# Value-side matrix of a cross-attention: fp16 high and low halves with three products in place of each fp32 product

## The reference, cut to what matters

```
vh = heads_split(v @ Wv)                 # v = ctx_1024, (2, 77, 256); 16 heads of 64
attn = softmax(dots)                     # dots: 1024 rows of each batch against 77 keys
out = einsum('bhij,bhjd->bhid', attn, vh)
out = out.transpose(0, 2, 1, 3).reshape(b, n, h * d)
out = out @ Wo + bo                      # Wo: (1024, 256)
```

## Time and profile before

| what | value |
|---|---|
| median of 3 runs | 427.75 us (427.56 to 428.26) |
| the profiled execution's own time | 428.12 us |
| its span, first to last instruction | 426.3 us |
| TensorE (PE) busy | 404.8 us, 95% of the span |
| VectorE (DVE) busy | 277.7 us, 65% |
| ScalarE (ACT) busy | 252.2 us, 59% |
| GpSimd (POOL) busy | 244.9 us, 57% |
| mean granted TensorE clock | 0.987 |

### The profile page before, as it was taken

How to read it: one execution, slowest core, us unless ns; L and a number is a source line. 1 busy time by engine, 2 the same in 40 slices (tenths; PEclk the granted TensorE clock), 3 DMA queues, 4 the chain that set the end, 5 groups by cost and what they waited for, 6 DMA issues and landing times.

```text
span 426.3 us, 10134 instructions
## 1 busy us (share of the span) xinstructions
PE 404.8 (95%) x3176; PEld 307.6 (72%) x3176; DVE 277.7 (65%) x684; ACT 252.2 (59%) x443; POOL 244.9 (57%) x213
## 2 busy tenths in 40 slices
PE   8899899999999999786999999999999999999991
PEld 8677577788877887674677777777777777777771
DVE  1777889899899989979688955444444444444340
ACT  3759889999899948444556444444444444444430
POOL 6536879998998865444054535445444444544242
PEclk9999999999999999989899999999999999999997
DMA  8992356566575624438767998888999888988753
GB/s 266 364 325 62 123 148 207 161 181 197 158 235 162 184 82 158 144 113 175 162 119 133 148 137 130 137 145 139 139 144 144 143 143 142 123 144 149 116 77 37
DMA packets 106241, 66.03 MB, mean 155 GB/s; under 512 B 80977, under 2 KB 99281, under 8 KB 106193
## 3 DMA queue, kind: packets, MB, share of 16 engines
q1 hardware_dynamic: 98512, 54.90, 55.2%
q0 software_dynamic: 7680, 10.49, 16.0%
HBM read 36.23 MB, written 9.96 MB: 108 GB/s over the span
## 4 chain that ended last, share of the span: by engine, by line
PE 58%; issue 16%; DMA 9%; DVE 6%; POOLq 3%; POOL 3%; ACT 2%; DVEq 0%; ACTq 0%
PE ps L816 14%; PE ps L648 12%; PE ps L618 11%; DMA out_rows<-work,idx_all 9%; PE ps L836 7%; PE ps L631 4%; POOLq L1707 3%; POOL work L1698 3%; PE ps L520 2%; PE ps L613 2%; PE ps L587 1%; PE ps L664 1%; PE ps L532 1%; DVE work L1136 1%; PE ps L602 1%
## 5 line engine op out<-in xcount | busy, mean ns | idle before, releaser
L816 PE MATMUL ps<-w_all,work 128*128 x960 | 151.4, 314 | 2.3 <-issue 2.3
L816 PEld LDWEIGHTS ps<-w_all,work 128*128 128x128 f16 x960 | 94.3, 99 | 48.9 <-issue 2.4
L1719 POOL DMA_INDIRECT out_rows<-work,idx_all x40 | 64.1, 1602 | 105.2 <-ACT work L1073 101.8
L1511 DVE SCALAR_TENSOR_TENSOR work<-ps,work 128x352 f32<-128x352 f32 x80 | 41.3, 523 | 66.9 <-PE ps L816 66.8
L836 PE MATMUL ps<-w_all,work 128*128 x681 | 80.8, 273 | 0.0
L836 PEld LDWEIGHTS ps<-w_all,work 128*128 128x128 f16 x681 | 66.4, 98 | 10.7 <-issue 0.2
L1636 POOL TENSOR_TENSOR w_all<-stage,w_all 128x1088 f16<-128x1088 f32 x30 | 67.6, 2256 | 9.2 <-ACT w_all L910 8.6
L1052 ACT ACTIVATE work<-ps 128x352 f32<-128x352 f32 x80 | 36.8, 463 | 54.0 <-PE ps L816 53.9
L1058 ACT ACTIVATE work<-work 128x704 f16<-128x704 f32 x39 | 30.8, 790 | 62.4 <-DVE work L1511 62.4
L1698 POOL DMA_INDIRECT work<-xn_rows,idx_all x40 | 41.2, 1029 | 29.0 <-issue 10.2
L618 PE MATMUL ps<-w_all 128*128 128x462 f16 (+1 forms) x288 | 57.4, 336 | 0.0
(11 more groups left out here) (159 smaller groups left out, 537.9 us busy)
## 6 DMA issues: line engine op xcount, KB each, us to landing
stage<-in_wt SPq DMA_DIRECT2D x36, 544.0 KB, 4.5
work<-in_x SPq DMA_DIRECT2D x30, 128.0 KB, 3.6
out_rows<-work SPq DMA_DIRECT2D x18, 128.0 KB, 4.4
xn_rows<-work SPq DMA_DIRECT2D x18, 128.0 KB, 4.4
w_all<-in_x SPq DMA_DIRECT2D x1, 1536.0 KB, 14.7
work<-work SPq DMA_TRANSPOSE x78, 3.7
w_all<-in_wk SPq DMA_DIRECT2D x2, 512.0 KB, 5.2
w_all<-in_wq SPq DMA_DIRECT2D x4, 256.0 KB, 7.0
```

What stands on the lines that cost most here:

```text
L816: mm = pe.matmul(ps[:, c, 0:half], xt[:, t % 2, block, :], weights(wbase + off, half), start=(k == 0 and n == 0), stop=(k == KD - 1 and n ...
L1511: dve.scalar_tensor_tensor(out=sg[:, t % 2, cols], in0=ps[:, 2 + c, 0:HID // 2], scalar=1.0 / SP_W, in1=sg[:, t % 2, cols], op0=ALU.mult, ...
L1719: pool.indirect_dma_start(out=acc, out_offset=bass.IndirectOffsetOnAxis(ap=idx_all[:, t:t + 1], axis=0), in_=yb[:, t % 2], in_offset=None, ...
```

## The change

The head values are kept as fp16 high and low halves `vz_h` and `vz_l`, in the bytes that `vz` had, and the output weights as `wo_h` and `wo_l` (64 times the weight, as fp16 high and low half). A product of B is then three fp16 products, high x high, low x high and high x low, issued one after the other. ScalarE rounds both halves of a pair (`v_high`, two instructions in place of one), VectorE subtracts for both (`v_low`, two instructions in place of one copy). ScalarE makes `wo_high(0)`, `wo_high(1)` (128 x 1024 each) and scales the bias in place, VectorE makes `wo_low(0)`, `wo_low(1)`. The scale 64 goes out of `b_high` and `b_low`. In step 0 of ScalarE `x_high(1)` stands ahead of `w_high(0)`.

```diff
         kt, o = pview(o, [PAIRS, B * J], F32)
-        vz, o = pview(o, [3, B, HJP], F32)
+        vz, _ = pview(o, [3, B, HJP], F32)
+        vz_h, o = pview(o, [3, B, HJP], F16)
+        vz_l, o = pview(o, [3, B, HJP], F16)
+        wo_h, o = pview(o, [INNER // P, D], F16)
+        wo_l, o = pview(o, [INNER // P, D], F16)
...
                 pe.wait_ge(wv_in[m // (PAIRS // 2)], 16)
-                for r in range(2):
-                    at_least(pe, v_half[r], m - 2)
+                at_least(pe, vl_ok, 2 * (m - 2))
                 head_values(wv_sb, m, V_BANKS[m % 3])
...
-                return pe.matmul(b_bank(k)[:, b], vz[rows, m % 3, b, cols], wo_sb[rows, m, :], start=start, stop=stop,
-                                 skip_group_check=True)
+                pairs = ((vz_h, wo_h), (vz_l, wo_h), (vz_h, wo_l))
+                for n, (v, w) in enumerate(pairs):
+                    mm = pe.matmul(b_bank(k)[:, b], v[rows, m % 3, b, cols], w[rows, m, :], start=(start and n == 0),
+                                   stop=(stop and n == len(pairs) - 1), skip_group_check=True)
+                return mm
...
-                for half in range(2):
-                    pe.wait_ge(wo_in[half], 16)
-                    pe.wait_ge(v_half[half], PAIRS)
+                pe.wait_ge(wo_lo_ok, 2)
+                pe.wait_ge(vl_ok, 2 * PAIRS)
                 even, odd = b_terms(2 * g, 0), b_terms(2 * g + 1, 1)
                 if g == 0:
-                    pe.wait_ge(bo_in, 16)
+                    pe.wait_ge(bo_ok, 1)
...
-            def v_even(m):
-                rows, j0 = slice(0, DH), head_col(2 * m)
+            def v_high(m):
                 act.wait_ge(kv_mm, PAIRS + m + 1)
-                act.activation(vz[rows, m % 3, :, j0:j0 + J],
-                               ps[rows, V_BANKS[m % 3], 0:B * J].rearrange("p (b j) -> p b j", b=B),
-                               ACT.Copy).then_inc(v_half[0], 1)
+                for r in range(2):
+                    rows, j0 = slice(r * DH, (r + 1) * DH), head_col(2 * m + r)
+                    act.activation(vz_h[rows, m % 3, :, j0:j0 + J],
+                                   ps[rows, V_BANKS[m % 3], 0:B * J].rearrange("p (b j) -> p b j", b=B),
+                                   ACT.Copy).then_inc(vh_ok, 1)
+
+            def wo_high(g):
+                act.wait_ge(wo_in[g], 16)
+                act.activation(wo_h[:, 4 * g:4 * g + 4], wo_sb[:, 4 * g:4 * g + 4], ACT.Copy, scale=SP_B).then_inc(wo_hi_ok, 1)
+
+            def bo_scale():
+                act.wait_ge(bo_in, 16)
+                act.activation(bo_b[:], bo_b[:], ACT.Copy, scale=SP_B).then_inc(bo_ok, 1)
...
                 if n == 0:
+                    wo_high(0)
+                    wo_high(1)
+                    bo_scale()
+                    x_high(1)
                     w_high(0)
-                    x_high(1)
                     b_high(0)
...
-            def v_odd(m):
-                rows, j0 = slice(DH, P), head_col(2 * m + 1)
-                dve.wait_ge(kv_mm, PAIRS + m + 1)
-                dve.tensor_copy(vz[rows, m % 3, :, j0:j0 + J],
-                                ps[rows, V_BANKS[m % 3], 0:B * J].rearrange("p (b j) -> p b j", b=B)).then_inc(v_half[1], 1)
+            def v_low(m):
+                for r in range(2):
+                    rows, j0 = slice(r * DH, (r + 1) * DH), head_col(2 * m + r)
+                    dve.wait_ge(vh_ok, 2 * m + r + 1)
+                    dve.tensor_tensor(vz_l[rows, m % 3, :, j0:j0 + J],
+                                      ps[rows, V_BANKS[m % 3], 0:B * J].rearrange("p (b j) -> p b j", b=B),
+                                      vz_h[rows, m % 3, :, j0:j0 + J], ALU.subtract).then_inc(vl_ok, 1)
+
+            def wo_low(g):
+                dve.wait_ge(wo_hi_ok, g + 1)
+                dve.scalar_tensor_tensor(out=wo_l[:, 4 * g:4 * g + 4], in0=wo_sb[:, 4 * g:4 * g + 4], scalar=SP_B,
+                                         in1=wo_h[:, 4 * g:4 * g + 4], op0=ALU.mult, op1=ALU.subtract).then_inc(wo_lo_ok, 1)
...
-                    dve.scalar_tensor_tensor(out=b_lo[:, :, c, :], in0=b_bank(k), scalar=SP_B, in1=b_hi[:, :, c, :],
-                                             op0=ALU.mult, op1=ALU.subtract).then_inc(b_lo_ok, 1)
+                    dve.tensor_tensor(b_lo[:, :, c, :], b_bank(k), b_hi[:, :, c, :], ALU.subtract).then_inc(b_lo_ok, 1)
...
             for m in (6, 7):
-                v_odd(m)
+                v_low(m)
+            for g in range(2):
+                wo_low(g)
```

More of the change, by code:

```diff
@@ L262, in build @@
         vz_ok, kv_mm, k_ok = (sem(n) for n in ("vz_ok", "kv_mm", "k_ok"))
-        v_half = sems("v_half", 2)
+        vh_ok, vl_ok, wo_hi_ok, wo_lo_ok, bo_ok = (sem(n) for n in ("vh_ok", "vl_ok", "wo_hi_ok", "wo_lo_ok", "bo_ok"))
         a_mm, a_hi_ok, a_lo_ok = sem("a_mm"), sem("a_hi_ok"), sem("a_lo_ok")
@@ L891, in b_high @@
                 for k in (2 * g, 2 * g + 1):
-                    act.activation(b_hi[:, :, B_CHUNKS[k], :], b_bank(k), ACT.Copy, scale=SP_B).then_inc(b_hi_ok, 1)
+                    act.activation(b_hi[:, :, B_CHUNKS[k], :], b_bank(k), ACT.Copy).then_inc(b_hi_ok, 1)
             def normalise(i):
@@ L1017, in _ @@
                 key_pair(m)
-            v_even(0)
+            v_high(0)
             normalise(0)
             key_pair(3)
-            v_even(1)
+            v_high(1)
             normalise(1)
@@ L1025, in _ @@
                 key_pair(m)
-                v_even(m - 2)
+                v_high(m - 2)
             for m in (6, 7):
-                v_even(m)
+                v_high(m)
             for n in range(NT):
@@ L1480, in _ @@
                 a_low(m)
-            v_odd(0)
+            v_low(0)
             a_low(3)
-            v_odd(1)
+            v_low(1)
             x_low(0)
@@ L1486, in _ @@
                 a_low(m)
-                v_odd(m - 2)
+                v_low(m - 2)
             for m in (6, 7):
-                v_odd(m)
+                v_low(m)
+            for g in range(2):
+                wo_low(g)
             dve.wait_ge(xall_in[1], 16)
```

## The result

The changed kernel is slower: 433.29 us median of 17 runs (430.04 to 434.63) against 428.54 of 17 runs of the kernel before (425.06 to 433.63), ratio 1.0116 with the interval 1.0088 to 1.0144. The forecast was 427.6 and no change, in a range of 427.2 to 429.0. The means of all 17 runs, 432.99 and 429.78, are 3.2 us apart, the medians 4.75.

What follows compares the result with a forecast made beforehand. Ahead of 48 us a chain of waits between TensorE, ScalarE and VectorE was taken to bound the kernel, then TensorE. Terms +0.20 + 0.10 - 0.42 = -0.12 us gave a 427.6 us median, range 427.2 to 429.0.

Steps and rivals of the forecast that it cites:

- The sum: Path terms at the end of the chain: +0.20 + 0.10 - 0.42 = -0.12 us.
- the preparation: Extra work ahead of make_b(0): +0.20 us for ScalarE's second v_high instruction, +0.10 for make_b(0) waiting for VectorE's wo_low.
- The products: TensorE's products of B: a pair falls from 0.432 to 0.327 us, saving 0.42 in make_b(0); other savings mostly hidden.
- The rival of a strict order: TensorE's products run in program order: a pair takes 0.436 us, make_b(0) costs 0.1 more; 428.15 us, chance 0.07.
- The upper bound, 0.40: VectorE's 64 x 154 subtraction ahead of make_b(0): one bounded between 0.24 and 0.40 us, 0.24 taken.
- The rival at 0.35: VectorE is late: subtractions cost 0.35 us, wo_low ends at 27.5, +0.35 on the sum; 428.0 us, chance 0.12.
- The wait ahead of L631: Sign that the forecast is right: this wait grows to over 2 us.
- the rival that I gave 0.25: TensorE's clock falls from 45.7 or 47.16 us on, losing 0.9 to 1.6 us, 1.2 taken; 428.8 us, chance 0.25.
- Carrying to the end: From 47.28 us on TensorE works without a gap that counts, so a shift there is carried to the end.

Runs made afterwards that it cites:

- the moved preparation: The changed kernel with its gaps filled and its preparation on ScalarE and VectorE reordered: 427.74 us; the same with three later gaps filled too: 427.66 us.
- the filled kernel: The changed kernel plus 40 small unused TensorE products behind make_b(4) and 16 ahead of prob_turn(0)'s last two transposes: 427.82 us, ratio 0.9982.

## Why the prediction was wrong, step by step

Two steps of it failed. The sum put the clock at nothing: what was saved in `make_b(3)` and `make_b(4)` "becomes idle time ahead of 45.11 and 47.28", and this idle time was taken to be free in the forecast, while it brought the clock to half speed for 6.8 us and cost 1.9 us in the trace. And the preparation was priced at +0.30, where it took 1.55.

- **The products: right.** Halves of the rows go on lying beside each other, -0.42 forecast for `make_b(0)`, -0.51 measured, and 1.44 of the saving of `make_b(3)` and `make_b(4)` hidden. The rival of a strict order wanted at least 1.85 us there (four pairs of 0.436 and one step more). The rule of the Trainium skill behind it ("TensorE: Matmul & The Clock Gate", Part 3), that matmuls start and end in program order, does not hold between the two halves of the rows here: 24 products of 0.109 in 1.49 us.
- **The preparation: too small by a factor of five.** I had +0.20 and +0.10; it was +1.55. The pieces, with the late start taken off: the wait at the first turn grew by 0.46 (two `v_high` in 0.64, not one more at 0.2). From there to the scores of tile 0 another 0.70 was lost: VectorE has no idle time from 19.13 on, `key_side` waits 0.17 for it, the last value products take 2.08 for 1.84, and its last low half of A ends at 24.40, just ahead of the scores at 24.45. The last 0.39 are those by which `v_low` and `wo_low`, over at 28.75 (28.26 without the late start, and not 27.05), come behind the turn of tile 1. The distance of 0.19 from the earlier trace rows was from a 64-row instruction starting in row 0 to one of 128 rows, 0.24 from the earlier trace rows between three copies on the same half. Neither row was of what the change adds: an instruction on the other half. I had called 0.24 "the row of the same size"; it was, but not of the same start. The upper bound, 0.40, would have held it (0.34), and with eight pairs it should have been carried to the end of the range of the sum. The rival at 0.35 had the price of one right and still let `wo_low` end at 27.5, since it did not carry the price through the pairs.
- **The wait ahead of L631: right** (over 2 us forecast, 2.34 measured), and so was the place from which it decides.
- **The clock: the rival that I gave 0.25 is what happened, and its time, 428.8, was too low by 4.5 us.** I argued from the earlier trace rows that the stretch would be emptier than one that preceded a fall, and set against it a stretch that was empty and kept 1.00. In the changed kernel the first was right; that the second can be right too is shown by the moved preparation, where one stretch did either. I gave the fall the length of the one at 182.7, 3.2 us, and priced it at 0.9 to 1.6; the one here lasted from 46.2 to 53.0, and cost 1.9. By the medians it is more still. Twice the missing clock times the span is the time spent at 1.2 GHz: on average 21.3 us of a run after, 12.9 before (99 runs), and 6.8 of these 8.4 us are the length of the one fall in the trace. Over the 99 runs of the kernel before, time and clock go together with a correlation of -0.93 and 3.8 us for 0.01 of clock. From 0.986 to 0.974 that would make 4.6 us of the 4.75 between the medians; with the 1.04 of the preparation it is more than the whole, so the two estimates don't add up exactly. That the clock is a cause and not a companion is shown for the 1.9 us ahead of 60 us, by the filled kernel. For the rest, some 1.8 us of the medians and 0.2 of the means, it is argued from the clock alone and not shown. What makes the clock of a later stretch fall in one run and not in the next I did not find out.
- **Carrying to the end: right.** What was late at 60 us was late at 417 (3.46 and 3.29).

## What to carry to other kernels

Work taken from TensorE in a place where it then waits is not free. Sum its busy time over the few microseconds around the wait, before and after; if another stretch of the trace as empty preceded a lower granted clock, put the fall into the sum with a chance of its own, and not only beside it. It is not certain even then, and single traces won't tell: compare the granted clock of many runs. Cheap products of a constant in the waits can be worth more than the change: in five waits of the kernel before they gave 0.7%, though the early two alone and the later three alone gave nothing that is clear of noise on the faster side. And take the price of a new instruction from a row whose predecessor starts on the same rows as the new one's will.

## What was not expected of the hardware

- In these traces ScalarE and VectorE both start an instruction on the other 64 rows only when the one before has ended, and one on the same rows about 0.1 us before that. After:

```profile
L888 ACT ACTIVATE w_all<-ps x16: 288/294/300, 14.8 to 24.8; 64x154 f16<-64x154 f32 x16
```

```profile
L1147 DVE TENSOR_TENSOR w_all<-ps,w_all x16: 300/318/327, 15.2 to 26.0; 64x154 f16<-64x154 f32 x16
```

These last 0.294 and 0.318 us, and stand 0.32 and 0.34 apart. For VectorE the Trainium skill says so ("VectorE: DVE Perf Modes", section "Two Vector instructions with no wait between them": an instruction that starts in another quadrant of 32 rows is held until the earlier ones are done), and the trace agrees; the prediction did not draw on it. For ScalarE only the trace shows it.
- The clock fell behind a stretch in which TensorE was idle for 2.34 us at the longest and busy for 4.24 of 6.20, and stayed at 1.2 GHz for 6.8 us although TensorE was then busy 6.16 of them. I had taken a fall for the answer to a stretch with less work in it, as at 179.3 (1.87 of 3.40), and its end for nearer, behind 3.2 us.
